# A Mamba layer and a mixture of experts on eight cores: router by quarters, three more expert units beside the scans, and the first half's sums ahead of the second half's experts

## Chip, cores and metric

One Trainium2 chip, eight NeuronCores, one sequence of 2048 tokens on each; the cores exchange nothing. The metric is the device time of the slowest core in microseconds.

## The reference

For each sequence (2048 tokens, width D = 1024):

```python
x = x + layernorm(mamba(layernorm(x)))
x = x + layernorm(moe(layernorm(x)))
# mamba: in-projection to 2 x 2048 channels, causal conv of 4 taps, silu;
#   h[t] = exp(dt[t]*A) * h[t-1] + dt[t]*x[t]*B[t]     (2048 channels x 16 states)
#   y[t] = sum over states of h[t]*C[t] + D*x[t];  y *= silu(z);  out-projection to 1024
# moe: logits = x @ router_W + router_b (15 experts); p = softmax(logits)
#   cw = p at its 3 largest entries, 0 elsewhere
#   out = relu(x @ sW1 + sb1) @ sW2 + sb2
#       + sum_e cw[:, e] * (relu(x @ eW1[e] + eb1[e]) @ eW2[e] + eb2[e])
```

## The kernel before

**Scans.** The sequence is worked in four quarters of 512 tokens, the 2048 channels in 16 groups of 128, the 16 states in fours: 64 steps a quarter, 256 in all (`LAST`). In a step ACT computes four exponentials (`dtexp`), DVE a product (`dbx`), one scan over four states (`scans`) and the product with C (`outer`), and PE adds the four states into one bank (`ysum`). Two buffers each are turned by `step % 2`. After every fourth step DVE closes a channel group (`yfin`).

**Order of the work.** All other work is placed by hand: `make_plan` puts tasks at steps, separately for each engine, and every engine runs its list strictly in order. Semaphores only make an engine wait. In a step ACT does `dtexp` first, PE `ysum` of the step before, DVE its small tasks and then the scan. In a quarter q stand the out-projection of quarter q-1 (`op`), its norms (`norm2`, `x2`, `norm3`), its transposes (`x3T`) and router logits, and the in-projections of the next quarter.

**Expert work.** A unit (`Unit`) is 256 rows through one expert's two matrices. The shared expert (number 15) has four units per half of the sequence; a routed expert (0 to 14) has one per half, of up to 256 gathered rows. A unit has eight large pieces, four `w1` (16 matmuls) and four `w2` (8 matmuls), and a routed one also two transposes of its gathered rows (`mT`). `make_units` deals the pieces to steps: `each(start, n)` gives n pieces a step before step 256 and one a step behind. Weights (four pieces of 1 MB) lie in one of four rooms (`buf`): 0 is `wa`, beside the scans the only one; 1 to 3 (`bcrep`, `xr`/`wr`, `zr`/`abv`) come free when the scans are over. A room's next weights are loaded when its last unit has used them, before step 256 on POOL's queue (L903), behind it on SP's (L706). POOL also gathers a unit's rows (`gather`, L875) and stores its output rows to `scr_y` (`store_y`, L910; L915 for shared units). ACT evicts `w2` into `ysc` (`ev_w2`, L1352), which waits until the store of the unit before has landed.

Experts 0 and 1 stand in the third quarter, 2 to 11 in the last, 12, 13 and 14 behind the scans with the last two shared units; then come the fifteen of the second half.

**Router.** It works per half of the sequence, 8 blocks of 128 tokens: `r_max` and `r_top` on DVE (L1003 to L1028: softmax, three largest, masks), `r_exp` on ACT, `rank` on PE (place of each token in its expert's list), `r_slot` on DVE (L1036 to L1050), and `scatter` on POOL (L885: 24 indirect DMAs that write token, weight and target to a slot table; L888 reads the table back into `sinfo`). In `r_top` each `max` and `max_index` waits for the one before it (`chain`).

**Sums.** `comb(h, b)` adds for a block of 128 tokens its three routed rows and the shared row (`cg`, 1 MB from `scr_y`) on PE (L1632), DVE and ACT make the norm (`st4`, `norm4`), and `fin` (L996) adds it to x2 (`xc`, 0.5 MB), which SP stores. The eight of the first half stand every three steps beside the first two experts of the second half, in two rooms and one pair of banks; those of the second half stand at the end, with three pairs of banks.

Of the kernel before, what the change touches and what calls it, by code (L numbers as in the profile page):

```python
# [15 lines left out]
D = 1024  # L16
# [10 lines left out]
HB = 8  # L27
# [38 lines left out]
def make_units():  # L66
# [80 lines left out]
def comb_steps():  # L147
    out = {}
    for b in range(8):
        out[(0, b)] = UNITS[E0].at[("w1", 0)] + 3 * b  # L150
        out[(1, b)] = END1 + 5 + b
    return out


def make_plan():
# [23 lines left out]
    for q in range(NQ + 1):  # L179
# [14 lines left out]
        if q == NQ:  # L194
            for tb in range(4):
# [13 lines left out]
            for tb in range(4):  # L209
                p.put(p.act, o + 5 + 2 * tb if tb < 2 else f + tb - 3, "norm3", q - 1, tb)  # L210
# [26 lines left out]
        if q in (2, 4):  # L237
            h = q // 2 - 1
            a = UNITS[shared(2 * q - 2)].at[("w1", 3)] + (5 if q == 2 else 6)
            b, c, d = (a + 3, a + 5, a + 6) if q == 2 else (a + 6, a + 8, a + 9)  # L240
            p.put(p.dve, a, "r_max", h)
            p.put(p.act, a + 1, "r_exp", h)
            p.put(p.dve, a + 2, "r_top", h)
            p.put(p.pe, b, "rank", h)
            p.put(p.act, b + 1, "ev_rank", h)
            for h_ in range(2 * h):
                p.put(p.pe, b, "cwT", h_)
                p.put(p.act, b + 1, "ev_cwT", h_)
            p.put(p.dve, c, "r_slot", h)
            p.put(p.pool, d, "scatter", h)  # L250
# [76 lines left out]
def build_program():  # L327
# [38 lines left out]
    with st:  # L366
# [167 lines left out]

        def usl(q, tb):
# [58 lines left out]
        LAST_F = max(n for task, n in od.f.items())  # L594


        def sp_prog(sy):
# [87 lines left out]
            def load_e(i, m, piece):  # L685
# [11 lines left out]
                else:  # L697
                    sy.wait_ge(p_y, LAST)
                    sy.wait_ge(p_f, od.f[("op", NQ - 1, 1, 3)] + 1)
                    if x.buf == 3 and m == 1:  # L700
# [30 lines left out]
            def load_cg(h, b):  # L731

                if h == 0:
                    if b < 2:
                        sy.wait_ge(p_y, LAST)
                    else:
                        sy.wait_ge(p_cb, b - 1)
# [122 lines left out]
        def pool_prog(g):  # L860
# [18 lines left out]
            def scatter(h):  # L879
                if h == 0:  # L880
                    g.wait_ge(d_zi, 32)
                g.wait_ge(v_slot, h + 1)
                for b in range(HB):
# [3 lines left out]
                g.wait_ge(d_sc, 24 * 16 * (h + 1))  # L887
                g.dma_start(sinfo[:, h], scr_si[h][0:NRT * 128, :].rearrange("(t p) c -> p t c", p=128)).then_inc(d_si, 16)  # L888
                g.wait_ge(d_si, 16 * (h + 1))
# [60 lines left out]
        def dve_prog(v):  # L950
# [48 lines left out]
            def r_max(h):  # L999
                v.wait_ge(a_tev, od.t[("logit", 2 * h + 1, 3)] + 1)  # L1000
                if h >= 1:
                    v.wait_ge(d_cw, 16 * h)
# [934 lines left out]
```

## Time and profile before

| | |
|---|---|
| median of 3 runs (lowest, highest) | 2727.54 us (2721.61, 2768.41) |
| profiled execution, time | 2716.03 us |
| its span, slowest core (cores 2698.0 to 2714.3) | 2714.3 us |
| busy: PE, DVE, ACT, POOL | 58%, 70%, 58%, 12% of the span |
| mean granted TensorE clock | 0.796 of full speed |
| HBM read and written | 202 GB/s over the span |

Busy shares are means over stages with different limits. Times within the trace count from the start of the span. A wait is put down to the semaphore that came last.

### The profile page before, as it was taken

The page shows a single profiled execution, that of the slowest core. Times are in us where ns is not written, and L with a number is a line of the kernel's source. Part 1 is how long each engine was busy: PE and PEld are TensorE (multiplying, and loading weights), DVE is VectorE, ACT ScalarE, POOL GpSimd, SP SyncE. Part 2 cuts the span into 40 slices and gives each one's busy share as a digit, 9 for nine tenths or more (in the row PEclk, how much of TensorE's full clock was granted, in tenths as well). Part 3 has the DMA queues.
Part 4 walks back from the last instruction along what each step waited for, and adds up shares of the span by engine and source line. Part 5 has one row for each costly group of instructions (what it writes and reads, how often), then busy time and mean ns, then how long its engine had stood idle before and what let it go on. Part 6 is the DMA issues. An engine that isn't in the chain of part 4 may idle for free.

```text
span 2714.3 us, 29033 instructions; the slowest of 8 cores (2698.0 to 2714.3 us)
## 1 busy us (share of the span) xinstructions
PE 1569.8 (58%) x7628; PEld 766.2 (28%) x7736; DVE 1909.0 (70%) x1490; ACT 1585.5 (58%) x2921; POOL 320.7 (12%) x290
## 2 busy tenths in 40 slices
PE   2625344543465545445645565556777777569995
PEld 1202111111132211112321232224444445326662
DVE  1197999997567999985789999979999941020003
ACT  4545666553468766546776676587777644234443
POOL 0000000000000000000007201001333203212220
PEclk9857577766787877767777788878998889689998
DMA  8399575777553443582211323242555487589975
GB/s 172 88 171 151 79 110 90 102 116 165 144 149 82 102 112 89 114 187 94 71 50 29 113 90 114 72 133 88 186 186 200 165 282 208 176 291 301 307 254 200
DMA packets 83695, 396.10 MB, mean 146 GB/s; under 512 B 21420, under 2 KB 30252, under 8 KB 55240
## 3 DMA queue, kind: packets, MB, share of 16 engines
q0 software_dynamic: 24544, 171.11, 30.0%
q1 hardware_dynamic: 58984, 223.05, 25.8%
q8 instruction: 70, 1.15, 0.2%
q14 instruction: 97, 0.79, 0.1%
HBM read 424.62 MB, written 123.64 MB: 202 GB/s over the span
## 4 chain that ended last, share of the span: by engine, by line
issue 35%; PE 22%; DMA 17%; DVE 15%; ACT 9%; POOL 1%; DVEq 1%; ACTq 0%; SPq 0%; POOLq 0%
PE ps_y L1564 6%; DVE abv L1100 6%; DVE hv L1089 4%; PE ps_c L1608 4%; PE ps_f L1479 4%; DMA xt<-x 3%; PE ps_a L1591 3%; DMA scr_y<-ysc,sinfo 3%; DMA bcrep<-scr_bc 3%; ACT abv L1374 2%; DMA wr<-scr_out 2%; DMA scr_x<-xt 2%; PE ps_f L1516 2%; DMA abv<-scr_y 1%; PE ps_f L1493 1%
## 5 line engine op out<-in xcount | busy, mean ns | idle before, releaser
L1089 DVE TENSOR_TENSOR_SCAN hv<-abv 128x2056 f16<-128x2056 f16 x256 | 1136.6, 4440 | 89.6 <-ACT abv L1374 71.4
L1374 ACT ACTIVATE abv<-ds,kc 128x512 f16<-128x512 f16 x1024 | 654.4, 710 | 72.8 <-DVE hv L1089 54.7
L1564 PE MATMUL ps_y<-abv,km 128*128 128x512 f16 x1024 | 356.1, 483 | 501.7 <-DVE abv L1100 500.1
L1079 DVE TENSOR_TENSOR abv<-ds,bcrep 128x2048 f16<-128x2048 f16 x256 | 309.2, 1208 | 51.6 <-PE ps_y L1564 27.3
L1100 DVE TENSOR_TENSOR abv<-hv,bcrep 128x2048 f16<-128x2048 f16 x256 | 312.1, 1219 | 6.4 <-DMA bcrep<-scr_bc 6.4
L1479 PE MATMUL ps_f<-xlnT,wr 128*128 128x512 bf16 x857 | 252.0, 448 | 80.2 <-ACT zr L1261 58.0
L1564 PEld LDWEIGHTS ps_y<-abv,km 128*128 128x128 f16 x1024 | 103.2, 111 | 684.4 <-issue 639.9
L986 DVE BATCH_NORM_STATS2 bst<-ps_f 128x6 f32<-128x512 f32 x11 | 7.7, 698 | 351.8 <-PE ps_f L1633 351.8
L1608 PE MATMUL ps_c<-wa,hT 128*128 128x512 bf16 x709 | 192.2, 424 | 45.8 <-ACT ysc L1352 25.4
L1340 ACT ACTIVATE hT<-ps_a,b 128x256 bf16<-128x256 f32 x304 | 126.2, 469 | 134.0 <-PE ps_a L1591 129.6
L1561 PE MATMUL ps_y<-xr,dd 128*128 128x512 f16 x64 | 32.7, 510 | 253.8 <-DVE zr L1107 253.8
L1479 PEld LDWEIGHTS ps_f<-xlnT,wr 128*128 128x128 bf16 x896 | 101.7, 115 | 234.1 <-issue 171.1
L1352 ACT ACTIVATE ysc<-ps_c,sinfo 128x512 bf16<-128x512 f32 x120 | 82.2, 686 | 146.0 <-PE ps_c L1608 92.1
L875 POOL DMA_INDIRECT xgu<-scr_x,sinfo x60 | 84.1, 1401 | 511.7 <-PE ps_t L1571 279.8
L1591 PE MATMUL ps_a<-xgu,wa 128*128 128x256 bf16 x1088 | 135.2, 285 | 2.7 <-ACT xgu L1331 1.5
L1516 PE MATMUL ps_f<-wr,zr 128*128 128x512 bf16 x435 | 112.8, 414 | 35.3 <-DMA wr<-scr_out 33.3
L1248 ACT ACTIVATE xr<-ps_f,kc 128x512 f16<-128x512 f32 x64 | 43.9, 686 | 141.5 <-PE ps_f L1493 141.5
L910 POOL DMA_INDIRECT scr_y<-ysc,sinfo x60 | 91.5, 1525 | 241.0 <-ACT ysc L1352 230.9
L937 POOL DMA_DIRECT2D scr_e<-e_w x30 | 15.1, 502 | 887.4 <-DVE abv L1100 887.4
L1591 PEld LDWEIGHTS ps_a<-xgu,wa 128*128 128x128 bf16 x1088 | 111.2, 102 | 30.1 <-issue 6.7
L1608 PEld LDWEIGHTS ps_c<-wa,hT 128*128 128x128 bf16 x736 | 77.5, 108 | 144.5 <-issue 81.2
L1074 DVE TENSOR_TENSOR ds<-ds,xr 128x512 f16<-128x512 f16 x64 | 25.9, 404 | 95.8 <-ACT ds L1366 95.8
(199 smaller groups left out, 2030.3 us busy)
## 6 DMA issues: line engine op xcount, KB each, us to landing
scr_e<-e_w POOLq DMA_DIRECT2D x30, 2048.0 KB, 19.9
wa<-scr_e POOLq DMA_DIRECT2D x56, 1024.0 KB, 6.4
wr<-scr_in SPq DMA_DIRECT2D x24, 1024.0 KB, 8.2
bcrep<-scr_e SPq DMA_DIRECT2D x24, 1024.0 KB
wa<-scr_e SPq DMA_DIRECT2D x20, 1024.0 KB
xt<-x SPq DMA_DIRECT2D x32, 512.0 KB, 5.7
bcrep<-scr_bc SPq DMA_DIRECT2D x32, 512.0 KB, 12.0
wr<-scr_out SPq DMA_DIRECT2D x14, 1024.0 KB, 7.8
```

The costliest lines, as they stand in the source:

```text
L875: g.indirect_dma_start(xg(a), None, scr_x3[x.half], bass.IndirectOffsetOnAxis(sinfo[:, x.half, 2 * x.expert + a, 0:1], 0)).then_inc(d_xg[a ...
L910: g.indirect_dma_start(scr_y[x.half], bass.IndirectOffsetOnAxis(sinfo[:, x.half, 2 * x.expert + rw, 2:3], 0), ysc[:, rw, :], None, bounds_ ...
L1079: v.tensor_mul(bv[:, step % 2, :, 2:T + 2], wdt[:, s_ % 2, :].unsqueeze(1).broadcast_to((128, 4, T)), brep[:, 4 * j:4 * j + 4, :]).then_in ...
L1089: v.tensor_tensor_scan(hv[:].rearrange("p n t -> p (n t)"), av[:, step % 2].rearrange("p n t -> p (n t)"), bv[:, step % 2].rearrange("p n ...
L1100: v.tensor_mul(bv[:, step % 2, :, 2:T + 2], hv[:, :, 2:T + 2], crep[:, 4 * j:4 * j + 4, :]).then_inc(v_hc, 1)
L1340: inst = s.activation(hT[:, hb, :], AB[c % 2][:, (hb % 2) * 256:(hb % 2 + 1) * 256], ACT.Relu, bias=b1[:, UNITS[i].expert, hb:hb + 1])
L1374: inst = s.activation(av[:, step % 2, n, 2:T + 2], dtv[:, s_ % 2, :], ACT.Exp, scale=k_a[:, g, 4 * j + n:4 * j + n + 1])
L1479: inst = t.matmul(ps[:], w[:, m, k, :], xlnT[:, k, :], start=(k == 0), stop=(k == 7))
L1516: inst = t.matmul(ps[:], zr[:, xs(q, g), tb * 128:(tb + 1) * 128], w[g // 8][:, g % 8, :], start=(g == 0), stop=(g == NG - 1))
L1564: inst = t.matmul(YB[:], k_eyh, bv[:, step % 2, n, 2:T + 2], start=False, stop=(j == 3 and n == 3))
L1591: inst = t.matmul(AB[c % 2][:, (hb % 2) * 256:(hb % 2 + 1) * 256], w[:, k, (hb % 4) * 128:(hb % 4 + 1) * 128], rows[:, k, :], start=(k == ...
L1608: inst = t.matmul(CB[rw][:], hT[:, k, rw * 128:(rw + 1) * 128], w[:, k, :], start=(k == 0), stop=(k == 7))
```

## The change

- The router works per quarter (4 blocks). Its tasks stand in the quarter behind: `scatter` at steps 91, 155, 217 and 279 instead of 155 and, for the second half, behind the scans. Within `r_top` four `max` are issued together, and four `max_index`. The slot table is read back after the second quarter of each half. The scatter of a quarter has 12 indirect DMAs.
- Experts 0 to 2 of the first half stand in the third quarter, 3 to 14 from step 213 at three pieces a step (before: 2, 2, 3), all in room 0. None is left behind the scans.
- Behind the scans come the last two shared units (steps 265 to 280, room 1), then the eight sums of the first half (281 to 288), then the fifteen experts of the second half from step 289. The transposes and norms of the last 512 tokens move up to between the last out-projections, and `x3t` of the last unit gets a room in `hv`.
- The sums have four rooms for `xc` and `cg` and three pairs of banks. SP issues the first four loads at step 265, each other one four sums later, when the result of its room is stored. `w1` of the first expert of the second half waits for all eight results (`v_out`).
- SP loads the weights of the first two second-half experts at steps 268 and 269, those of room 3 all behind the last sum.

```diff
@@ make_units
-    run([(0, e, 0, 0) for e in range(2)], each(128 + 37, 1))
+    run([(0, e, 0, 0) for e in range(3)], each(128 + 37, 1, 1, 1, 1, 2))
     run([(1, 15, 0, 0)], each(192 + 13, 2))
     run([(1, 15, 1, 0)], each(192 + 17, 2))
-    s = run([(0, e, 0, 0) for e in range(2, 12)], each(192 + 21, 2, 2, 3))
-    s = run([(0, 12, 0, 1)], each(max(s, LAST + 9), 1))
-    s = run([(1, 15, 2, 2)], each(s, 1))
-    s = run([(1, 15, 3, 2), (0, 13, 0, 0), (0, 14, 0, 1)], each(s, 1))
-    run([(1, e, 0, (0, 2, 1, 3)[e % 4]) for e in range(NE)], each(s, 1))
+    s = run([(0, e, 0, 0) for e in range(3, NE)], each(192 + 21, 3))
+    s = run([(1, 15, 2, 1)], each(max(s, LAST + 9), 1))
+    s = run([(1, 15, 3, 1)], each(s, 1))
+
+    run([(1, e, 0, (0, 2, 1, 3)[e % 4]) for e in range(NE)], each(s + 8, 1))
@@ comb_steps
-        out[(0, b)] = UNITS[E0].at[("w1", 0)] + 3 * b
+        out[(0, b)] = UNITS[E0].at[("mT", 0)] - 8 + b
@@ make_plan, last quarter, and the router
+                p.put(p.act, t + 3, "norm3", q - 1, tb)
                 f = UNITS[S14].at[("w1", 0)]
-                n = (f - 3 + tb) if tb < 2 else f + 2 + tb
+                n = o + 6 + tb if tb < 2 else f - 3 + 3 * tb
...
+        if q >= 1:
+            f = UNITS[shared(2 * q - 2)]
+            a = f.at[("w1", 3)] + 5 if q < NQ else f.at[("w1", 0)] + 9
+            p.put(p.dve, a, "r_max", q - 1)
+            p.put(p.act, a + 1, "r_exp", q - 1)
+            p.put(p.dve, a + 2, "r_top", q - 1)
+            p.put(p.pe, a + 3, "rank", q - 1)
+            p.put(p.act, a + 4, "ev_rank", q - 1)
+            p.put(p.dve, a + 5, "r_slot", q - 1)
+            p.put(p.pool, a + 5 + (q < NQ), "scatter", q - 1)
@@ banks, load_xc, load_cg
-            return FB if h == 0 else (FB, CB, AB)[b % 3]
+            return (FB, CB, AB)[b % 3]
...
+                    elif b < 4:
+                        sy.wait_ge(p_y, LAST)
+                        sy.wait_ge(p_f, od.f[("op", NQ - 1, 1, 3)] + 1)
                     else:
-                        sy.wait_ge(d_xc[b - 2], 48)
+                        sy.wait_ge(d_xc[b - 4], 48)
...
-                        sy.wait_ge(p_cb, b - 1)
+                        sy.wait_ge(p_cb, b - 3)
@@ scatter
-            def scatter(h):
+            def scatter(q):
+                h, b0 = q // 2, 4 * (q % 2)
...
-                g.wait_ge(v_slot, h + 1)
-                for b in range(HB):
+                g.wait_ge(v_slot, q + 1)
+                for b in range(b0, b0 + 4):
                     for k in range(3):
                         g.indirect_dma_start(scr_si[h], bass.IndirectOffsetOnAxis(sli[:, h, k, b:b + 1], 0),
                                              info[:, k, b, :], None).then_inc(d_sc, 16)
-                g.wait_ge(d_sc, 24 * 16 * (h + 1))
...
+                if q % 2 == 1:
+                    g.wait_ge(d_sc, 24 * 16 * (h + 1))
@@ r_top
-                for b in range(HB):
-                    chain(v.max(m8[:, b, :], pr[:, b, :]))
-                    chain(v.max_index(ix[:, b, :], m8[:, b, :], pr[:, b, :]))
...
+                for b in range(b0, b0 + 4):
+                    inst = v.max(m8[:, b, :], pr[:, b, :])
+                chain(inst)
+                for b in range(b0, b0 + 4):
+                    inst = v.max_index(ix[:, b, :], m8[:, b, :], pr[:, b, :])
+                chain(inst)
@@ w1 on PE
+                if i == E0 and c == 0:
+                    t.wait_ge(v_out, 8)
@@ SP's order behind the scans
-                            at = op_end if (u.buf, m) != (3, 1) else comb_steps()[(0, 7)] + 1
+                            at = op_end if u.buf != 3 else comb_steps()[(0, 7)] + 1
+                        if i == E0:
+                            at = UNITS[S14].at[("w1", 0)] + 3
+                        elif i == E0 + 1:
+                            at = UNITS[S14].at[("w1", 0)] + 4
...
-            put_moe(s_ - 1 if h == 0 else last_z.at[("w2", 1, 1)] + 2, "xc", h, b)
-            put_moe(s_ - 1 if h == 0 else END1 + 3, "cg", h, b)
+            soon = UNITS[S14].at[("w1", 0)] if b < 4 else comb_steps()[(h, b - 4)] + 4
+            put_moe(soon if h == 0 else last_z.at[("w2", 1, 1)] + 2, "xc", h, b)
+            put_moe(soon if h == 0 else END1 + 3, "cg", h, b)
```

## Rows read from the trace of the kernel before

**Rows 1.** DVE's timeline, closing products of two scan groups (start us, us)

```profile
2020.00 0.68 DVE L1107 TENSOR_TENSOR zr<-ps_y,zr 128x512 f16<-128x512 f32 x1
...
2048.60 0.69 DVE L1107 TENSOR_TENSOR zr<-ps_y,zr 128x512 f16<-128x512 f32 x1
```

**Rows 2.** Waits of PE, 1895 to 2180 us (total us, times, longest)

```profile
PE ps_y L1564 <- DVE abv L1100: 46.4, 24, 4.3
PE ps_y L1561 <- DVE zr L1107: 18.7, 8, 4.4
```

**Rows 3.** Windows: length, busy us (instructions) by engine, TensorE clock, DMA share, GB/s

```profile
2000.00:2050.00 50.00, 39.26 (x257) 23.82 (x258) 49.00 (x33) 39.83 (x71) 16.67 (x13) 1.00 0.53 182
...
2100.00:2150.00 50.00, 36.81 (x224) 22.26 (x224) 49.24 (x32) 33.65 (x63) 9.90 (x11) 0.88 0.55 196
...
2220.00:2250.00 30.00, 22.66 (x172) 16.18 (x175) 3.37 (x8) 16.51 (x34) 1.50 (x2) 0.83 0.98 334
...
2290.00:2330.00 40.00, 12.14 (x39) 4.50 (x41) 0.00 (x0) 4.72 (x7) 20.43 (x22) 0.62 0.40 86
...
2510.00:2530.00 20.00, 17.83 (x131) 11.77 (x131) 0.00 (x0) 8.50 (x15) 3.98 (x4) 1.00 1.00 310
```

**Rows 4.** PE's timeline: first projection, and w1 and last w2 of units

```profile
2187.57 3.61 PE L1516 MATMUL ps_f<-wr,zr 128*128 128x512 bf16 x15 [1.01 <-DVE zr L1107]
...
2349.72 2.76 PE L1591 MATMUL ps_a<-xgu,wa 128*128 128x256 bf16 x16 [1.47 <-ACT xgu L1331]
...
2468.39 7.15 PE L1591 MATMUL ps_a<-xgu,zr 128*128 128x256 bf16 x64
...
2599.73 7.15 PE L1591 MATMUL ps_a<-xgu,zr 128*128 128x256 bf16 x64
...
2655.68 6.85 PE L1608 MATMUL ps_c<-bcrep,hT 128*128 128x512 bf16 x31 [1.46 <-ACT hT L1340]
```

**Rows 5.** POOL's timeline: first and last scatter (of 24) of either router, next store

```profile
1433.78 4.91 POOL L885 DMA_INDIRECT scr_si<-info,sli  x1 [12.33 <-DVE info L1044]
...
1492.04 4.04 POOL L885 DMA_INDIRECT scr_si<-info,sli  x1 [0.30 <-issue]
...
2282.65 1.01 POOL L885 DMA_INDIRECT scr_si<-info,sli  x1 [0.30 <-issue]
...
2311.82 0.96 POOL L885 DMA_INDIRECT scr_si<-info,sli  x1 [0.30 <-issue]
...
2323.32 0.59 POOL L915 DMA_DIRECT2D scr_y<-ysc  x1 [7.16 <-DMA sinfo<-scr_si]
```

**Rows 6.** Wait of the sums; w2 pieces, y sum; DMA issues (last: us to landing)

```profile
PE ps_f L1632 <- DMA abv<-scr_y: 30.5, 5, 11.2
...
1971.29 5.30 PE L1608 MATMUL ps_c<-wa,hT 128*128 128x512 bf16 x16
1977.29 1.03 PE L1564 MATMUL ps_y<-abv,km 128*128 128x512 f16 x4 [0.70 <-DVE abv L1100]
...
wa<-scr_e POOLq DMA_DIRECT2D x56, 1024.0 KB, 6.4
...
zr<-scr_x SPq DMA_DIRECT2D x4, 512.0 KB, 26.5
```

**Rows 7.** DVE's timeline: the second half's router, borders of its three parts

```profile
2266.36 0.28 DVE L1011 TENSOR_REDUCE rsum<-pr 128x8 f32<-128x120 f32 x1 [5.71 <-ACT pr L1312]
...
2267.44 0.18 DVE L1015 MAX8 m<-pr 128x8 f32<-128x15 f32 x1
...
2268.07 0.18 DVE L1015 MAX8 m<-pr 128x8 f32<-128x15 f32 x1
...
2274.84 0.28 DVE L1028 TENSOR_TENSOR pr<-sls,pr 128x120 f32<-128x120 f32 x1
2276.61 0.22 DVE L1036 TENSOR_SCALAR slm<-rkc 128x120 f32<-128x120 f32 x1 [1.48 <-ACT rkc L1318]
...
2281.20 0.14 DVE L1050 TENSOR_SCALAR some<-big 1x1 int32<-1x1 f32 x1
```

More of the change, by code:

```diff
@@ L236, in make_plan @@
             p.put(p.act, o + 62, "siluz", q + 1, 0)
[L237 to L250, printed above, removed]
+        if q >= 1:
[8 more added lines that the diff above has]
+            p.put(p.pool, a + 5 + (q < NQ), "scatter", q - 1)
+    for h in range(2):
+        n = LAST - 26 if h == 0 else UNITS[E0].at[("w2", 0, 0)]
+        p.put(p.pe, n, "cwT", h)
+        p.put(p.act, n + 1, "ev_cwT", h)
     for step, t in PIECES:
@@ L592, in e_done @@
             return (d_ep if early(i) else d_e[UNITS[i].buf])[2 * m + piece]
-        LAST_F = max(n for task, n in od.f.items())
         def sp_prog(sy):
@@ L699, in load_e @@
                     sy.wait_ge(p_f, od.f[("op", NQ - 1, 1, 3)] + 1)
-                    if x.buf == 3 and m == 1:
+                    if x.buf == 3:
                         sy.wait_ge(p_cb, 8)
@@ L997, in fin, with r_max @@
                 inst.then_inc(v_out, 1)
[L999 to L1002, printed above, removed]
[L1003 to L1017 removed]
+            def r_max(q):
+                bs = slice(4 * (q % 2), 4 * (q % 2) + 4)
+                v.wait_ge(a_tev, od.t[("logit", q, 3)] + 1)
+                if q >= 2:
+                    v.wait_ge(d_cw, 16)
+                chain(v.reduce_max(nmx[:, bs], lg[:, bs, :], AX.X, negate=True))
+                v.tensor_add(pr[:, bs, :], lg[:, bs, :], nmx[:, bs].unsqueeze(2).broadcast_to((128, 4, NE))
+                             ).then_inc(v_rmx, 1)
@@ new lines, in r_top @@
+            def r_top(q):
+                h, b0 = q // 2, 4 * (q % 2)
+                bs = slice(b0, b0 + 4)
+                v.wait_ge(a_rex, q + 1)
+                if q >= 1:
+                    v.wait_ge(p_t, od.t[("rank", q - 1)] + 1)
+                chain(v.reduce_sum(rsum[:, bs], pr[:, bs, :], AX.X))
+                chain(v.reciprocal(rsum[:, bs], rsum[:, bs]))
+                chain(v.tensor_mul(pr[:, bs, :], pr[:, bs, :], rsum[:, bs].unsqueeze(2).broadcast_to((128, 4, NE))))
+                if q >= 2:
+                    v.wait_ge(d_si, 16)
+                for b in range(b0, b0 + 4):
[4 more added lines that the diff above has]
+                chain(inst)
+                chain(v.tensor_copy(ixf[:, bs, :], ix[:, bs, 0:3]))
@@ L1023, in r_top @@
[L1023 to L1038 removed]
+                chain(v.tensor_add(sls[:, bs, :], oh[:, 0, bs, :], oh[:, 1, bs, :]))
@@ new lines, in r_top, with r_slot @@
+                chain(v.tensor_add(sls[:, bs, :], sls[:, bs, :], oh[:, 2, bs, :]))
+                v.tensor_copy(mk[:, bs, :], sls[:, bs, :]).then_inc(v_msk, 1)
+                v.memset(cwm[:, h, bs, 15:16], 1.0)
+                v.tensor_mul(cwm[:, h, bs, 0:NE], sls[:, bs, :], pr[:, bs, :]).then_inc(v_cw, 1)
+                v.wait_ge(v_cw, q + 1)
+                v.tensor_mul(pr[:, bs, :], sls[:, bs, :], pr[:, bs, :]).then_inc(v_cwf, 1)
+            def r_slot(q):
+                h, b0 = q // 2, 4 * (q % 2)
+                bs = slice(b0, b0 + 4)
+                v.wait_ge(a_tev, od.t[("rank", q)] + 1)
+                v.wait_ge(v_cw, q + 1)
+                v.wait_ge(v_cwf, q + 1)
+                rank = rkc[:, 0:128].rearrange("p (b e) -> p b e", e=16)[:, bs, 0:NE]
+                chain(v.tensor_scalar(slm[:, bs, :], rank, CAP - 0.5, 8192.0, AL.is_gt, AL.mult))
+                chain(v.tensor_add(sls[:, bs, :], rank, k_ios.unsqueeze(1).broadcast_to((128, 4, NE))))
+                chain(v.tensor_max(slm[:, bs, :], slm[:, bs, :], sls[:, bs, :]))
@@ L1584, in w1 @@
                     t.wait_ge(a_fev, od.f[("x3T", n // 2, 2 * (n % 2) + 1)] + 1)
-                rows = xgT if x.routed else x3t
+                rows = xgT if x.routed else x3r(4 * x.half + x.part)
                 if 4 * i + c >= 2:
```

142 lines of the change are left out of this document (65 added, 77 removed).

## The prediction, made before the changed kernel ran

> **What bounds the kernel now.** I read the page's 40 slices, then the windows by stage, then the timeline of each engine around the stage borders, then the waits. They show three stages.
>
> Up to about 2187 us the state scans run, and DVE sets the pace. In the last quarter four scan steps take 28.6 us, 7.15 us a step [rows 1], without a gap. PE is not full: in 285 us it waits 46.4 and 18.7 us for DVE, some 1.65 us a step [rows 2], though a window there has it busy 39.3 of 50 us [rows 3].
>
> From the first output projection (2187.57) to the first expert matmul of the second half (2349.72) are 162.1 us [rows 4]. PE does seven units of work there, but for 40 us it is busy 12 [rows 3]: POOL scatters the second half's routing between 2282.65 and 2312.8, reloads the slot table and only at 2323.3 stores the next expert output [rows 5]. ACT waits for that store before it may overwrite `ysc`, and PE waits for ACT.
>
> From 2349.72 to 2662.5 run the fifteen experts of the second half, 312.8 us. The last twelve have nothing between them: eight of them take 131.3 us (16.42 each, DMA share 1.00 and 310 GB/s), the last four 62.8 (15.7 each) [rows 3, 4]. The first three take 118.7 us, because eight sums (`comb`) of the first half stand between them, and PE waits 30.5 us for their data [rows 4, 6]. Then come 51.8 us of the second half's sums.
>
> **Part 1: routers beside the scans.** Before, one 8-block router (first half) lies beside the scans and one behind. Afterwards three 4-block ones lie beside them and one behind. An 8-block router costs DVE 0.7 us (`r_max`, two of its instructions), 8.8 (`r_top`, 2266.36 to 2275.1) and 4.7 (`r_slot`, 2276.61 to 2281.3), 14.2 together [rows 7]. In it each block's max and index take 0.63 us with their waits, 5.0 for eight. With 14 of 16 waits gone I take the bare 0.44 us (0.18 plus 0.26), 1.8 for four. The other 9.2 us are waits and tiny instructions at half the elements: between half (4.6) and unchanged (9.2); I take 7.2, near unchanged, since 0.18 us for 15 elements beside 0.28 for 120 is mostly fixed cost. So 9.0 us each (6.4 to 11.7), 27 for three, less the 14.2 removed: **+13 us** (+5 to +21) on the bound engine.
>
> **Part 2: the scatter of the third quarter on POOL's queue.** It stands at step 217, in the middle of dense units. Beside scans 24 scatters took from 1433.8 to 1496.1, 2.6 us each; behind them 24 took 30.1, 1.26 each [rows 5]. So 12 take about 31 us, started as scan 216 starts (call this 0). Behind them on POOL stand the two output stores of unit 9, the last weight piece of unit 10 and gathers and weights of unit 11. ACT's eviction of unit 10 (step 219) waits for unit 9's store to land, and stands on its engine ahead of the exponentials for scan 220, which is due at 28.6. Scatters end at 32 (quicker once DVE stalls), store issued at 34, landed about 38, eviction 0.7, exponentials 4.3: scan 220 starts at 43. **+14 us**. Unit 10's last weights, issued at 36 and landing in the usual 6.4 us [rows 6], come at the same moment. Bounds: 0 if scatters go at 1.26 us (15 us in all is covered), 25 if also the weights behind run late. The same scatter at step 91 and the shorter one at 155 have no near unit behind them: nothing.
> The Trainium skill (SBUF — State Buffer, "SBUF: two separate sides") has DVE and GpSimd share a port pair under an exclusive lock, so that GpSimd can't write descriptors while certain DVE operations run, and gives 620 ns grown to about 3100. The trace agrees in kind: scatters of 4 to 4.9 us stand among those of 0.96. By the page's figure for all twelve POOL would be blocked 41 us, and the stall some 7 us longer.
>
> **Part 3: three more units beside the scans.** One of them is in the third quarter, where PE waits more. In steps 213 to 252 there are 12 units for 10, three pieces a step. PE needs 12 x 15.7 for units, 41 for the y sums of 40 steps (1.03 each [rows 6]) and 14 for the z projections: 244 of 286 us at full clock. The 1.65 us of waiting a step shrink to about 0.6. Where z projections stand (8 steps) a step needs 7.1, all there is, but PE may lag 3.4 us before DVE feels it. I take **+4 us** (0 to +30; the upper end if every step of that stretch slips by the missing eviction latency of 0.8 us).
> Sum of the scan stage: **+31 us**, so the first output projection starts at 2218.6.
>
> **Part 4: from there to the second half's experts, 132 instead of 162 us.** Call the start 0. Eight projections of 3.5 us [rows 4] and two waits for the norms (no unit covers them now: transposes are due between them) end at 33; PE comes out of a pause, so add 3 for half clock. The two shared units, 14 us each, run to about 68 with the router between them. Its chain: last logit 51, exp 55, `r_top` to 60, rank, `r_slot` to 66, 12 scatters of 1.26 us to 81, reload (before: 11.5 us from the last scatter to the next store) to 93, gathers and transposes: 104. That alone would let the experts start at 104.
> But `w1` of the first one now also waits for all eight sums, and these wait for transfers. A sum reads 1.57 MB. SP issues four sums' loads at 28 to 34, then weights of units 23 and 24 (8.4 MB), of 25 (4.2), then four results (2.1), each of which must have landed before its room takes the next sum's 1.57 MB. With the last four sums' loads (6.3), a part of the first four's, stores and gathers some 31 MB must pass after 34. Direct loads ran at 334 GB/s [rows 3]: 93 us, so the last sum's data land at 127, plus product, statistics and result (8 us) is 135; some 3 MB may have passed before 34, hence **132**. Bounds: 104 if the sums are never late, 150 if landing round trips leave queue gaps of 3 us each. An SP transfer behind weights did land late before: 26.5 us for the 0.5 MB of `zr<-scr_x` [rows 6].
> The Trainium skill (DMA: Bandwidth & Descriptors, "Queues, rings and completion order") has the queue rows served in turn by packets and a ring's descriptors consumed in order. So small loads on POOL's queue would get past SP's weights, and the sums' loads on SP's own would not; both are as I reckon here.
> Gain: **30 us**. The old 40 us hole is gone, since no unit with a `ysc` store stands behind the scatter but unit 22's own.
>
> **Part 5: fifteen experts without sums between them.** The state at their start is that of 2468: three weight rooms full, the fourth loading. So 11 at 16.42 and 4 at 15.7: 243.4 us for 312.8, **-69 us**. Bounds: 236 (all 15.7) to 258 (17.2, where DMA at 305 GB/s carries a unit's 5.24 MB). The end, 51.8 us, is not touched.
>
> **Sum.** +31 -30 -69 = -68 us. The profiled execution has a span of 2714.3 and a time of 2716.0: 2648. The three runs' median is 11.5 us above that execution and their lowest 5.6; I add 6: **2654 us**.
>
> **Rivals.**
> A. *The sums are not late; the router's chain sets the start (104).* For: DMA share was only 0.40 in the old hole, queues can run empty. Against: 31 MB. It gives 28 us less, 2626.
> B. *Transfers and density take more*: start at 150, a unit 17.2 us or the scan stage another 15 us: 2654 + 18 + 15, about 2687. For: share 1.00 in all late windows. Against: 12 units did run at 16.2 in it.
> C. *Slower: PE becomes the bound of the last scan quarter.* One mechanism: half clock. Two w2 pieces took 5.3 us at a low clock against 3.4 [rows 6]. 244 us of work fill the 286 at a mean clock of 0.86; below that the scans wait for the y sums. All 99 us gained behind the scans, less the 27 of parts 1 and 2, are lost at 244/c = 286 + 72, c = 0.68; at 0.65 the time is about 2740. For: 0.88 in one window before [rows 3]. Against: PE kept 1.00 in the densest window, and denser work leaves fewer pauses.
> D. *The scatter does not hold up the scans*, because POOL gets its port during other DVE gaps: 14 us less, 2640; inside my range.
>
> **Chances and range.** Forecast with D 0.52, A 0.17, B 0.24, C 0.07. Range 2600 to 2710: A with some of the other lower bounds, B with the upper bound of part 3. A measurement of this kernel tells about 2% from no change; that is 2673 and 2782. The forecast falls to "within 2%" in a sixth of its cases, A never, B mostly: faster 0.63, same 0.32, slower 0.05.
>
> **What would show it.** Right: the first projection near 2219; three router groups of about 9 us on DVE beside scans; one DVE wait of 10 to 20 us for ACT's exponentials near step 220; PE idle ahead of sums 4 to 7 on DMA; first expert at 130 us behind the first projection, and waiting for a result of DVE, not for the gather; experts at a pitch of 15.7 to 16.6 us with DMA at 1.00. Wrong: many small DVE waits for PE's y sums in the last quarter (C), experts starting with their gather (A), or a pitch above 17 us (B).

## The result, and the profile after

The changed kernel took 2696.9 us (median of five runs) beside 2721.6 us for the kernel before on the same chip: ratio 0.9906, 95% interval 0.9877 to 0.9935. It is 25 us faster where 73 were forecast. That lies inside the range of 2600 to 2710, but short of the 2% that the chance of 0.63 stood on. One of the five executions of either kernel, and some of the experiments', were in a slower state, in which the cores of one die show a lower clock; the ratios, and the times of the experiments below, leave these out.

The granted clock and the span of three of the cores, after the change, first:

```profile
core 0: 2657.4 us, clock 0.795
...
core 4: 2695.1 us, clock 0.792
...
core 6: 2654.4 us, clock 0.798
```

Before, the eight spans lay between 2698.0 and 2714.3; now they lie between 2654.4 and 2695.1. The mean core gained 32.2 us (2706.2 to 2674.0), the slowest 19.2. The clock did not move (0.796 before and 0.792 after on the slowest core). Since the cores of one run already differ by up to 30 us at scan 84, where both kernels are the same, I read the stretches below as means over the eight cores. "Scans 212 to 224" is from the start of one scan to that of the other; "first sum" (its first matmul), "last sum" (start of its second product) and "first expert" (first `w1` of unit 23) count from the core's first output projection of the last quarter; "units" is from the first expert to the last `w2`.

| us, mean of 8 cores | before | after | difference |
|---|---|---|---|
| scans 84 to 96 (router of quarter 0) | 85.6 | 93.8 | +8.2 |
| scans 144 to 160 (router of quarter 1; before, of the half) | 149.8 | 144.3 | -5.5 |
| scans 212 to 224 (router and scatter of quarter 2) | 85.7 | 111.4 | +25.7 |
| scans 224 to 255 | 220.9 | 228.9 | +8.0 |
| first projection | 2182.2 | 2215.1 | +32.9 |
| from there to the last sum | 265.5 | 156.0 | |
| from there to the first expert | 164.9 | 166.2 | +1.3 |
| units | 308.1 | 241.9 | -66.2 |
| tail of PE's work | 38.1 | 37.3 | -0.8 |

So the scans lost about what was forecast (+33 for +31), the experts gained what was forecast (-66 for -69), and the stretch between them, from which 30 us were to come, gave nothing. A part of the +33 is chance: from scan 84 to scan 255 the kernel after takes 36.7 us more, but its cores reached scan 84 3.8 us earlier (843.3 for 847.1), up to where both kernels are the same.

**The scans.** POOL's timeline of core 4 at scan 216, start and length in us, operation, and in brackets the idle time before and its releaser:

```profile
1923.09 1.53 POOL L898 DMA_INDIRECT scr_si<-info,sli  x1 [0.30 <-issue]
1924.93 4.56 POOL L898 DMA_INDIRECT scr_si<-info,sli  x1 [0.30 <-issue]
...
1949.04 0.96 POOL L898 DMA_INDIRECT scr_si<-info,sli  x1 [0.31 <-issue]
1950.31 1.00 POOL L925 DMA_INDIRECT scr_y<-ysc,sinfo  x1 [0.30 <-issue]
...
1956.37 0.58 POOL L918 DMA_DIRECT2D wa<-scr_e  x1
```

ACT's timeline in the same place:

```profile
1956.62 0.69 ACT L1384 ACTIVATE ysc<-ps_c,sinfo 128x512 bf16<-128x512 f32 x1 [15.26 <-DMA scr_y<-ysc,sinfo]
```

PE's timeline, where the weights issued by POOL behind the stores are late too:

```profile
1960.49 3.57 PE L1646 MATMUL ps_c<-wa,hT 128*128 128x512 bf16 x8 [13.76 <-DMA wa<-scr_e]
```

DVE's timeline, with the product that the next scan group begins with:

```profile
1958.90 0.42 DVE L1101 TENSOR_TENSOR ds<-ds,xr 128x512 f16<-128x512 f16 x1 [15.98 <-ACT ds L1398]
```

This is Part 2 as forecast: twelve scatters take 27 us, the store of unit 9's output is issued at 1950.3, ACT's eviction waits for its landing until 1956.6, and DVE, which had no gap in [rows 1], stands 16 us for ACT. The scatters took between 0.96 and 4.56 us, as in [rows 5], and ended in a row of 0.96 once DVE stood still. What holds a long one is seen beside DVE's scan:

```profile
1931.12 4.44 DVE L1116 TENSOR_TENSOR_SCAN hv<-abv 128x2056 f16<-128x2056 f16 x1
```

```profile
1932.15 4.17 POOL L898 DMA_INDIRECT scr_si<-info,sli  x1 [0.30 <-issue]
```

Three scatters were begun while a scan ran (1924.93, 1932.15, 1939.17), and each ended 0.8 us behind the end of that scan (1928.69, 1935.56, 1942.91).

Behind scan 224 DVE stands three more times for PE, which it never did there before the change. Here it is on core 2, PE's timeline and then DVE's:

```profile
2062.32 4.42 PE L1646 MATMUL ps_c<-wa,hT 128*128 128x512 bf16 x10 [5.23 <-DMA wa<-scr_e]
```

```profile
2071.16 1.23 DVE L1106 TENSOR_TENSOR abv<-ds,bcrep 128x2048 f16<-128x2048 f16 x1 [5.76 <-PE ps_y L1600]
```

PE comes late with the y sum, because it waited for weights (`wa`) that POOL issued. This happens near steps 225, 235 and 245 on most cores; DVE's waits of this kind are 3.5 us in the mean of the cores (0.6 to 8.4; 1 us more is a wait at the same instruction on cores 4 and 7 to which the profile gives no releaser). With 2.0 us for ACT just behind step 235 on every core and about 1 us of shorter waits they make up the +8.0.

**The gap between scans and experts.** PE's timeline of core 4, from the first projection to the first expert:

```profile
2231.50 5.50 PE L1548 MATMUL ps_f<-wr,zr 128*128 128x512 bf16 x15 [1.40 <-DVE zr L1134]
...
2278.36 3.57 PE L1629 MATMUL ps_a<-x3t,bcrep 128*128 128x256 bf16 x16 [4.45 <-ACT hT L1372]
...
2361.61 1.87 PE L1665 MATMUL ps_c<-abv,km 128*128 128x512 bf16 x4 [27.97 <-DMA abv<-scr_y]
...
2385.26 1.25 PE L1665 MATMUL ps_c<-zr,km 128*128 128x512 bf16 x4 [2.49 <-DMA zr<-scr_y]
...
2397.27 9.93 PE L1629 MATMUL ps_a<-xgu,wa 128*128 128x256 bf16 x64 [1.46 <-ACT xgu L1363]
```

SP's DMA queue in the same time (weights, first results, and the loads that stand behind them):

```profile
2283.80 2.70 SPq L713 DMA_DIRECT2D wa<-scr_e  x4
2286.70 5.36 SPq L713 DMA_DIRECT2D xr<-scr_e  x2
...
2307.16 11.58 SPq L713 DMA_DIRECT2D bcrep<-scr_e  x2
2328.61 3.47 SPq L761 DMA_DIRECT2D out<-ds  x2
2352.99 0.33 SPq L739 DMA_DIRECT2D ds<-scr_x  x1
...
2369.43 0.34 SPq L761 DMA_DIRECT2D out<-xr  x1
2369.96 0.32 SPq L739 DMA_DIRECT2D zr<-scr_x  x1
...
2375.83 0.34 SPq L761 DMA_DIRECT2D out<-ds  x1
2376.36 0.32 SPq L739 DMA_DIRECT2D xr<-scr_x  x1
```

and the windows (length, busy us and instructions of PE, its weight loads, DVE, ACT and POOL, TensorE clock, DMA share, GB/s):

```profile
2300.00:2320.00 20.00, 17.36 (x107) 8.04 (x108) 6.41 (x35) 4.94 (x13) 9.21 (x10) 0.91 0.98 224
2320.00:2340.00 20.00, 6.74 (x18) 1.55 (x16) 8.96 (x18) 6.64 (x13) 4.07 (x4) 0.61 1.01 320
2340.00:2360.00 20.00, 0.00 (x0) 0.00 (x0) 0.00 (x0) 0.00 (x0) 3.12 (x4) 0.50 0.93 258
2360.00:2380.00 20.00, 10.45 (x25) 2.50 (x25) 6.04 (x12) 3.70 (x8) 0.00 (x0) 0.59 0.76 253
2380.00:2400.00 20.00, 11.26 (x46) 4.96 (x47) 7.44 (x14) 5.61 (x10) 1.89 (x2) 0.59 0.71 216
2400.00:2500.00 100.00, 93.12 (x693) 64.57 (x698) 0.00 (x0) 48.98 (x87) 23.87 (x24) 0.99 0.99 314
```

Result 0 is issued at 2328.61, behind 12.6 MB of weights (units 23, 24 and 25) on the same queue. Until it has landed its room may not take sum 4's input, and that load is next in SP's order: it goes out at 2352.99, 24.4 us later. PE, DVE and ACT do nothing at all between 2340 and 2360. What follows is a chain of round trips, not a stream: 8.6 us until sum 4 can start (2361.61), then result 3, which `fin` writes on DVE behind the statistics of sum 4. DVE's timeline:

```profile
2366.13 0.70 DVE L1001 BATCH_NORM_STATS2 bst<-ps_c 128x6 f32<-128x512 f32 x1 [28.80 <-PE ps_c L1666]
...
2367.95 1.41 DVE L1011 SCALAR_TENSOR_TENSOR xr<-ps_f,mv,xr 128x512 f32<-128x512 f32 x2
```

so it is issued at 2369.43, with sum 6's load behind it. Sum 7's load needs result 3's room, but that had landed at 2372.44; what it waits for is its turn on SP behind result 4, which DVE finished only at 2375.75, behind the statistics of sum 5. It goes out at 2376.36 and takes 8.9 us (2385.26). The DMA share falls to 0.76 and 0.71: here the queues wait, the bytes don't.

The router's chain was slower too. POOL's timeline behind the scans, to set beside the last lines of [rows 5]:

```profile
2333.34 1.68 POOL L902 DMA_DIRECT2D sinfo<-scr_si  x1 [10.34 <-issue]
...
2347.92 1.12 POOL L930 DMA_DIRECT2D scr_y<-ysc  x2 [12.90 <-DMA sinfo<-scr_si]
```

POOL waits 10.3 us between the last scatter and the reload, which may not start before the scatters have landed, and 12.9 for the table; before, the table took 7.16 [rows 5].

### The profile page after: what moved, and what is told of

It is laid out like the page before. It is cut to its first block, busy times and chain, and to the rows that moved or that the text cites. A ratio compares the mean times of both kernels' runs of the same rounds, so it can differ in the third digit from the quotient of the medians.

```text
span 2695.1 us, 29141 instructions; the slowest of 8 cores (2654.4 to 2695.1 us)
## 1 busy us (share of the span) xinstructions
PE 1561.3 (58%) x7632; PEld 762.5 (28%) x7736; DVE 1914.5 (71%) x1546; ACT 1585.9 (59%) x2925; POOL 369.7 (14%) x302
## 4 chain that ended last, share of the span: by engine, by line
issue 32%; PE 23%; DMA 17%; DVE 14%; ACT 10%; POOL 1%; DVEq 1%; ACTq 0%; SPq 0%; another core or an unknown queue 0%; POOLq 0%
PE ps_y L1600 6%; DVE abv L1127 5%; PE ps_a L1629 5%; DVE hv L1116 4%; PE ps_f L1511 4%; DMA scr_y<-ysc,sinfo 4%; DMA xt<-x 4%; PE ps_c L1646 3%; ACT abv L1406 2%; PE ps_f L1548 2%; DMA wr<-scr_out 2%; DMA bcrep<-scr_bc 2%; DMA scr_x<-xt 1%; DMA wa<-scr_e 1%; DVE h_last L1125 1%
## 5 line engine op out<-in xcount | busy, mean ns | idle before, releaser
L1646 PE MATMUL ps_c<-wa,hT 128*128 128x512 bf16 x773 | 200.3, 411 | 47.4 <-DMA wa<-scr_e 25.2
L887 POOL DMA_INDIRECT xgu<-scr_x,sinfo x60 | 99.3, 1656 | 473.9 <-PE ps_t L1607 319.4
L1629 PE MATMUL ps_a<-xgu,wa 128*128 128x256 bf16 x1216 | 145.1, 279 | 5.9 <-ACT xgu L1363 2.9
L1548 PE MATMUL ps_f<-wr,zr 128*128 128x512 bf16 x435 | 117.7, 429 | 36.7 <-DMA wr<-scr_out 33.8
L1629 PEld LDWEIGHTS ps_a<-xgu,wa 128*128 128x128 bf16 x1216 | 120.8, 100 | 32.2 <-issue 9.3
L925 POOL DMA_INDIRECT scr_y<-ysc,sinfo x60 | 101.9, 1699 | 160.6 <-ACT ysc L1384 148.4
## 6 DMA issues: line engine op xcount, KB each, us to landing
bcrep<-scr_bc SPq DMA_DIRECT2D x32, 512.0 KB, 12.5
```

The source lines that it names most:

```text
L887: g.indirect_dma_start(xg(a), None, scr_x3[x.half], bass.IndirectOffsetOnAxis(sinfo[:, x.half, 2 * x.expert + a, 0:1], 0)).then_inc(d_xg[a ...
L925: g.indirect_dma_start(scr_y[x.half], bass.IndirectOffsetOnAxis(sinfo[:, x.half, 2 * x.expert + rw, 2:3], 0), ysc[:, rw, :], None, bounds_ ...
L1548: inst = t.matmul(ps[:], zr[:, xs(q, g), tb * 128:(tb + 1) * 128], w[g // 8][:, g % 8, :], start=(g == 0), stop=(g == NG - 1))
L1629: inst = t.matmul(AB[c % 2][:, (hb % 2) * 256:(hb % 2 + 1) * 256], w[:, k, (hb % 4) * 128:(hb % 4 + 1) * 128], rows[:, k, :], start=(k == ...
L1646: inst = t.matmul(CB[rw][:], hT[:, k, rw * 128:(rw + 1) * 128], w[:, k, :], start=(k == 0), stop=(k == 7))
```

## The experiments

Theory A: the sums' loads are held in SP's order, behind result 0 and result 3. Theory B: transfers as such (bytes) set the end, wherever they stand. For the scans: the scatter on POOL's queue (12 to 16 us) against denser units.

**e1: the third quarter's scatter behind the scans** (it loses no order that a reader of it needs; the table of the half is read only there).

```
-p.put(p.pool, a + 5 + (q < NQ), "scatter", q - 1)
+p.put(p.pool, LAST - 2 if q == 3 else a + 5 + (q < NQ), "scatter", q - 1)
```

> The changed kernel with one edit: the 12 scatters of the third quarter stand at step 254 instead of 217, behind the last unit's output stores. Theory (POOL's queue holds up the scans): the 16.6 us that steps 216 to 220 lost against the kernel before shrink to under 3 us, scan 255 starts 14 to 18 us earlier (near 2206 instead of 2222), all behind it moves up unchanged, time 14 to 18 us shorter, about 2680. Rival (the loss at these steps comes from the denser units, and the scatter only stands beside it): scan 255 moves by less than 5 us, time unchanged.

Measured: scans 212 to 224 take 98.9 us for 111.4, the first projection is at 2202.1 for 2215.1, everything behind it nearly as in after (first expert 168.1 for 166.2). Two executions took 2682.1 and 2699.2 us, without an interval, so the stretches carry the reading: the scatter cost 12.5 us, a little less than the 14 to 18 expected. DVE's wait of 16 us fell, in the timeline of e1's slowest core, to

```profile
1940.05 0.42 DVE L1101 TENSOR_TENSOR ds<-ds,xr 128x512 f16<-128x512 f16 x1 [1.43 <-ACT ds L1398]
```

Scans 224 to 255 stayed at 230.0: their 8 us are no echo of the scatter.

**e2: sums 4 to 7 four steps later**, so that result 3 is written before sum 4's statistics stand on DVE.

```
-run([(1, e, 0, ...) for e in range(NE)], each(s + 8, 1))
+run([(1, e, 0, ...) for e in range(NE)], each(s + 12, 1))
-out[(0, b)] = UNITS[E0].at[("mT", 0)] - 8 + b
+out[(0, b)] = UNITS[E0].at[("mT", 0)] - 12 + b + 4 * (b >= 4)
```

> The changed kernel with sums 4 to 7 and all behind them four steps later in the written order (no work added), so that on DVE the results of sums 0 to 3 no longer stand behind the statistics of sum 4, and SP can store them. Theory A (SP's queue order alone: the first result lands 24 us late behind expert weights): the hole ahead of sum 4 stays near 28 us, and the first expert starts at most 5 us earlier than 165.8 us behind the first projection. Theory B (the circle result 3 - statistics of sum 4 - loads of sum 6 on SP adds to it): the hole ahead of sum 4 stays, but sum 7 comes 12 to 16 us earlier and the first expert starts near 152 us.

Measured: one run, 2687.0 us; first expert 161.1 for 166.2. The order on DVE costs 5 us, no more. (Kernels that are the same in this stretch agreed within 2 us: 166.2 in after and 168.1 in e1, 138.9 in both e5 and e6.)

**e3: weights of units 24 and 25 issued behind the last sum's loads.** The same bytes, in another order on SP's queue.

```
 elif i == E0 + 1:
-    at = UNITS[S14].at[("w1", 0)] + 4
+    at = comb_steps()[(0, 7)]
+elif i == E0 + 2:
+    at = comb_steps()[(0, 7)]
```

> The changed kernel with SP's loads of the weights of units 24 and 25 (8.4 MB) moved behind the loads of the last sum; order of the sums as in the changed kernel. Theory A (results of the sums land late behind 8.4 MB of weights on the same queue): result 0 lands within 8 us instead of 24, the hole ahead of sum 4 falls from 28 to under 10 us, the first expert starts at 135 to 145 us behind the first projection instead of 165.8, then set by the router's chain or the circle on DVE. Rival C (the router's chain sets the start, with the gathers issued at 118 us): no earlier than 160. Rival D (DMA volume sets it): weights only move behind, the first two experts then wait for their weights by what was gained, and the end stays within 8 us.

Measured: one run, 2678.8 us; last sum at 139.3 for 156.0, first expert 149.5 for 166.2, units 244.4 for 241.9. PE's wait for sum 4 fell from 27.97 us, in PE's timeline of e3, to

```profile
2342.85 1.86 PE L1665 MATMUL ps_c<-abv,km 128*128 128x512 bf16 x4 [11.45 <-DMA abv<-scr_y]
```

On that core sum 4's load went out 3.7 us behind the issue of result 0, where it took 24.4 before. Just short of what was expected (135 to 145), with the same bytes in another order: theory A for 17 us, and B is out. No run put the weights on another queue, so whether result 0 landed late by its place in SP's queue or because all queues were full stays open; e3 shows that issuing 8.4 MB later mends it.

**e4: e2 and e3 together.**

> Both edits of the two kernels above. If they are independent links of one chain of transfers: first expert at 120 to 132 us behind the first projection, set by the router's chain (slot table, gather, transposes), and the time 30 to 40 us shorter than the changed kernel's. If volume is the bound: the expert starts earlier but waits for weights, time at most 15 us shorter.

Measured: 2678.3 us, ratio 0.981 (0.972 to 0.990); first expert 144.2, the sum of both gains (22.0 for 5.1 + 16.7), not the 120 to 132 that was expected. The time is 19 us under after's, where 30 to 40 were expected. Units 246.9: 5 us are given back, since three rooms of weights are no longer full at their start; on the slowest core PE waits 8.3 us there for weights, in after not at all.

**e5: eight rooms for eight sums.** Sums 4 to 7 get memory that is idle by then (`xlnT`, `xt`, `xr`, `wr`), so that no load waits for a result; weights of units 24 and 26 wait for the sums.

```
+if b >= 6:
+    return xt[:, b - 6, :]
+if b >= 4:
+    return xlnT[:, 4 * b - 16:4 * b - 12, :]...
...
-    sy.wait_ge(d_xc[b - 4], 48)
+    sy.wait_ge(v_x2, 16)
```

> The changed kernel with eight rooms instead of four for the first half's sums (xc 4 to 7 in xlnT and xt, cg 4 to 7 in xr and wr), all loads issued by step 268, so that no load waits for a result to land; in exchange the weights of unit 24 (room 2) load behind the sums, as those of unit 26 do. Theory (the start of the second half's experts was set by round trips of room reuse on SP's queue): PE never waits ahead of sums 4 to 7 for data, the last sum starts at 105 to 115 us behind the first projection instead of 156, and the first expert at 120 to 130 us instead of 166.2, now set by the router's chain (gathers issued near 115). Units take 3 to 8 us more (245 to 250 us), time 30 to 38 us under the changed kernel's. Rival (volume of transfers): the sums' data still come late, first expert not before 145 us, time at most 20 us shorter.

Measured: 2676.3 us, ratio 0.9834 (0.9809 to 0.9859). The last sum is at 109.0, as expected, and none waits for data any more. But the first expert is at 138.9 where 120 to 130 was expected: behind the sums stands now what the sums had hidden. So the time is 21 us under after's, not the 30 to 38 expected.

**e6: e5 and e1 together.**

> Eight rooms for the sums, and the 12 scatters of the third quarter at step 254 instead of 217. Both causes removed, they lie in different stages: the gains add, 13 us in the scans (mean of the cores, as measured with the scatter alone) and 30 to 38 behind them: 43 to 50 us under the changed kernel, about 2650, ratio to the kernel before near 0.973. If they share a cause, the sum is less than 35.

Measured: 2663.7 us, ratio 0.9785 (0.976 to 0.981), less than expected but faster than both kernels: scans 212 to 224 99.5, first expert 138.9. The total, 33 us under after, is below the 35 that I had named as the sign of a common cause, but by stretches both gains are there in full (12 us in the scans as in e1, 27 to the first expert as in e5); it was e5's own gain that I had put too high. What holds the first expert is seen in PE's timeline of its slowest core, whose sums ended near 2342:

```profile
2357.20 1.01 PE L1615 MATMUL ps_t<-km,xgu 128*128 128x128 bf16 x8 [14.84 <-DMA xgu<-scr_x,sinfo]
```

and in POOL's:

```profile
2304.73 1.00 POOL L906 DMA_INDIRECT scr_si<-info,sli  x1 [11.05 <-DVE info L1077]
...
2318.31 0.96 POOL L906 DMA_INDIRECT scr_si<-info,sli  x1 [0.27 <-issue]
2328.65 1.68 POOL L910 DMA_DIRECT2D sinfo<-scr_si  x1 [9.38 <-DMA scr_si<-info,sli]
2343.16 1.12 POOL L938 DMA_DIRECT2D scr_y<-ysc  x2 [12.83 <-DMA sinfo<-scr_si]
2344.56 1.00 POOL L895 DMA_INDIRECT xgu<-scr_x,sinfo  x1 [0.29 <-issue]
```

This is rival A's chain (scatter, table, gather), at 139 us and not at 104.

**e7: unit 14 left behind the scans**, in after otherwise; what one unit beside the scans costs there, and saves.

```
-run([(0, e, 0, 0) for e in range(3, NE)], each(192 + 21, 3))
+run([(0, e, 0, 0) for e in range(3, NE - 1)], each(192 + 21, 3))
+run([(0, NE - 1, 0, 0)], each(max(s, LAST + 9), 1))
```

> The changed kernel with expert 14 of the first half taken from beside the scans and put behind them, ahead of the two shared units; 11 instead of 12 units at three pieces a step. If the denser units themselves cost the scans the 8 us of steps 224 to 255 evenly, these steps take 226 to 228 us instead of 228.9 (220.9 before). If the loss comes from single late stores and weights in POOL's queue, it stays at 228 to 230. In either case the first sum comes 12 to 17 us later behind the first projection, since the unit needs 15.7 us there, and the time is 10 to 15 us longer than the changed kernel's: the price of one unit left behind.

Measured: one run, 2737.4 us, 40 more than after where 10 to 15 were expected. Scans 224 to 255 take 230.3, not less: the 8 us there are not an even price of density. The first sum comes 22.4 us later (104.2; 12 to 17 were expected) and the first expert 36.9 (203.1). On the slowest core sum 4's load goes out 34.5 us behind the issue of result 0 (2358.45 to 2392.90), 10 us more than in after. PE's timeline of e7, at sum 4:

```profile
2400.20 1.86 PE L1666 MATMUL ps_c<-abv,km 128*128 128x512 bf16 x4 [43.13 <-DMA abv<-scr_y]
```

Taking one unit away from beside the scans gave them nothing back, and behind them it cost, as this kernel is ordered, more than twice its own 16 us.

**e8, e9, e10: is the router's chain slow because the queues are full?** Theory S: yes; rival F: an indirect write and a table of small rows take that long by themselves. e8 is e6 with unit 25's weights issued behind the last sum; e9 moves unit 23's as well (8.4 MB out of the chain's way); e10 is e8 again, for its time.

```
 e8:  +elif i == E0 + 2:
      +    at = comb_steps()[(0, 7)] + 1
 e9:  -if i == E0:
      -    at = UNITS[S14].at[("w1", 0)] + 3
      -elif i == E0 + 2:
      +if i in (E0, E0 + 2):
```

> Kernel: e6 with one thing moved: the 4.2 MB of weights of unit 25 (the third expert of the second half) are issued behind the last sum, after those of unit 24, and no longer while the router's chain runs. What sets the first expert at 139 us behind the first projection in e6 is POOL's chain: last scatter issued, 9.4 us until it has landed, 12.8 us for the table, then some 12 us to the gathered rows. Before the change, in a window where the DMA engines were busy 0.40, the same two waits took 1.7 and 7.2 us. Theory S: the saturated queues (share 0.96 to 1.00) lengthen them, so with 4.2 MB less in the way (13 us at 320 GB/s) the share falls below 0.9 for some 10 us, the two waits fall by 5 to 10 us together and the first expert starts at 127 to 134 (mean of the cores). Rival F: the landings' length has nothing to do with SP's weights (a fixed latency of an indirect write and of small rows): waits stay at 9 and 13 us, first expert at 137 to 140. Either way the units may take 1 to 4 us more (246 to 250), since a room is filled later, so the total moves by less than 0.3%: ratio 0.975 to 0.979.

> Kernel: e8, and the 4.2 MB of unit 23 (the first expert of the second half) issued behind the last sums as well, so that 8.4 MB less than in e6 run beside the router's chain. It is made to see POOL's two waits, mean of the eight cores: behind the last scatter (3.4 us before the change, 10.6 in e6, 9.7 in e8) and for the table (7.4, 13.8, 11.0). Theory S (saturated queues lengthen them): e8 left the DMA share near 1.00 in most cores, so it shortened them little; with 25 MB of transfers between 35 and 115 us cut to 17 MB (0.65 of what 320 GB/s carry) the waits fall to at most 7 and 9, gathers are issued at 105 to 112 instead of 117 to 121. Rival F (a fixed latency): 9 to 11 and 11 to 14, gathers as in e8. The first expert itself then waits for unit 23's weights, which are issued at about 105 and need 13 us and more: it starts at 125 to 138 by S, 130 to 145 by F, and unit 24's weights come later, so the units may take 2 to 6 us more. Ratio 0.972 to 0.981.

> Kernel: e8 unchanged, for its time, since its first three rounds gave no interval. By the stretches of its trace (first projection at 2203.9, first expert 133.6 behind it, units 243.7, mean of the cores) it should be 7 to 8 us under e6 and 0.3% under it: ratio 0.973 to 0.978, about 2650 us. If the 5 us that the first expert gained are only noise between runs, the ratio is 0.978 and more.

| us, mean of 8 cores | before | after | e6 | e8 | e9 |
|---|---|---|---|---|---|
| POOL's wait behind the last scatter | 3.4 | 11.0 | 10.6 | 9.7 | 3.5 |
| its wait for the table | 7.4 | 12.3 | 13.8 | 11.0 | 6.9 |
| first gather | | 119.4 | 121.1 | 117.1 | 106.8 |
| first expert | 164.9 | 166.2 | 138.9 | 133.6 | 125.3 |
| units | 308.1 | 241.9 | 246.1 | 243.7 | 254.8 |

POOL's timeline of e9's slowest core:

```profile
2306.89 0.96 POOL L906 DMA_INDIRECT scr_si<-info,sli  x1 [0.27 <-issue]
2311.12 1.68 POOL L910 DMA_DIRECT2D sinfo<-scr_si  x1 [3.27 <-DMA scr_si<-info,sli]
2319.83 1.12 POOL L938 DMA_DIRECT2D scr_y<-ysc  x2 [7.03 <-DMA sinfo<-scr_si]
```

and the windows of that core at the same time:

```profile
2290.00:2310.00 20.00, 18.21 (x76) 6.37 (x74) 11.62 (x35) 8.09 (x17) 11.57 (x12) 1.00 0.61 223
2310.00:2330.00 20.00, 8.44 (x33) 2.52 (x31) 14.37 (x28) 9.08 (x20) 4.78 (x5) 0.80 0.82 192
```

With DMA shares of 0.61 and 0.82 both waits are back where they were before the change, where the share was 0.40 [rows 3]. Theory S holds, and F is out: the two waits are 24.4 us in e6 and 10.4 in e9. e8 alone would not have told it: it left the share near 1.00, and the waits fell by 3.7 us where S wanted 5 to 10, though the first expert came at 133.6, within S's 127 to 134. e9 itself gives 8.7 of its 13.6 us back, for the units start with empty rooms and take 254.8; two executions took 2645.5 and 2646.5 us, without an interval. e8 starts the first expert later and keeps its units short: as e10 it took 2647.7 us, ratio 0.9741 (0.9716 to 0.9766), with the first expert at 134.0 again. e9 and e10 can't be told apart (2631.1 and 2631.4 us in the mean of their cores); both are under e6 (2639.7).

## Why the prediction was wrong

- **Part 1 (routers, +13).** Right. `r_max`, `r_top` and `r_slot` of four blocks took 0.5, 4.4 and 3.8 us, 8.8 for 9.0. By stretches +8.2 and -5.5, and some 8 of the +25.7, 11 in all.
- **Part 2 (scatter, +14).** Right in size and by its own steps; e1 took 12.5 us away. Rival D is out: POOL did not find its gaps. The Trainium skill's page "SBUF — State Buffer", section "SBUF: two separate sides", has its lock between DVE and GpSimd; the trace agrees in kind, with scatters of 4.17 to 4.56 us that end 0.8 us behind a scan, and of 0.96 as soon as DVE stood. The 7 us more that its figure would have made were not there: the stall was 16 on the slowest core.
- **Part 3 (density, +4).** Low: about 13 (8.0 behind scan 224, and 5 of the 25.7, which is the difference to parts 1 and 2), inside its bounds. (Its 0.6 us of waiting left a step is 42 us over 40 steps, so 1.05; the sum doesn't use it.) e1 and e7 show that it is neither the scatter's echo nor even. From 1895 to 2200 PE waits 25.2 us for weights in POOL's queue, where it waited for none before:

```profile
PE ps_c L1646 <- DMA wa<-scr_e: 25.2, 4, 13.8
```

  13.8 of them belong to the scatter. The others are the waits near steps 225, 235 and 245, behind each of which DVE stands for the late y sum. That they go away with earlier weights wasn't tried.
- **The stage as a whole.** Parts of 13, 14 and 4 were forecast, and some 11, 12.5 and 13 came: 36.7 us for 31. That the first projection stood at +33 is due to the cores' 3.8 us at scan 84, by luck.
- **Rival C.** Out as it was meant: the clock from scan 213 to 255 was 0.90 to 0.93 on the eight cores, before 0.89 to 0.92. But its sign, DVE waiting for y sums, did appear, for 3.5 us in the mean behind scan 224, and came from late weights.
- **Part 4 (132 instead of 162).** This is the step that failed: 166. It priced the sums' data as a volume, 31 MB at 334 GB/s, in which each transfer moves up when its turn comes. SP's queue was not a volume but an order with holds in it. (1) Sum 4's load stood behind the landing of result 0, and that behind 12.6 MB of weights issued shortly before; moving 8.4 of them gave 17 us back in e3. (2) Results 3 and 4, with loads behind them on SP, stood behind the statistics of sums 4 and 5 on DVE: 5 us by e2, which takes only result 3 out of this. I had even written that each result "must have landed before its room takes the next sum's 1.57 MB", and had put queue gaps of 3 us each into the upper bound. The one hold behind result 0 was 24.4 us, and loads then took 8.6 and 8.9 us until their sum could start, one behind the other. The upper bound of 150 was too low for that. Of the 34 us that were missed, 27 are the sums' (e5 has the first expert at 138.9) and 7 the router's chain. The sum itself had a slip too: 3 MB at 334 GB/s are 9 us, so its own terms give 126 and not 132, further off.
- **Part 4, the router's chain (104).** Wrong as well, and hidden by the sums. e9, with everything else out of its way, starts the first expert at 125. On e9's slowest core its steps read: last projection done at 39 (36 in my chain), last logit at 64 (51), first scatter at 79 (66), last one begun at 92 (80), table there at 105 (93), first `w1` at 124 (104). So the router began 13 us late: 3 us were lost in the projections, and about 10 in the first shared unit, in which the last two transposes stand and PE waits 4.5 us for `hT` (the first product's output, which ACT writes); and gathers, transposes and evictions took 19 us and not 11. With full queues the two landings add 14 us more (24.4 in e6 for 10.4 in e9): 139, as in e5 and e6. I had reckoned that POOL's small transfers get past SP's weights; they took more than twice as long beside them. So even with sums that are never late the forecast of 132 was out of reach for the kernel as it was written, and rival A's 28 us were worth nothing.
- **Part 5 (units, -69).** Right: -66.2, at 16.1 us a unit with the DMA share at 0.99 in 2400 to 2500.
- **The mark of the first expert.** I had it waiting for a result of DVE. On PE it waits for ACT's copy of the transposed rows; these transposes stand behind the last sum in PE's order. The last sum set the time all the same.
- **The core.** All terms were reckoned on the core that ended last. By the mean of the cores the result is -32.2 us, which is the sum of the table (+32.9 +1.3 -66.2 -0.8 = -32.8); the measure takes the slowest, and the spread went from 16 to 41 us. Why it grew isn't settled.

## What to carry to other kernels

When a queue works in order and one of its transfers waits for a room, reckon the time to that point from the landing of what frees the room, with all bytes issued ahead of it, and only then add bytes: 8.4 MB of weights that nobody needed yet, issued 42 to 10 us before a 0.5 MB result, cost 17 us here, and e3 had them back by order alone. A small, serial chain of DMAs (scatter, table, gather) pays for full queues with its latency at each link, so bulk loads that can wait go behind it, but no more of them than the next stage can do without: e9 started its first expert 8.3 us before e8 and took 11.1 us more for the units. And when one thing is late, work out what would be next without it before counting the gain; here it was 139 us behind 166, where I had believed 104.

## What was not expected of the hardware

- POOL's two waits, for twelve indirect writes to land and for the table of small rows, were 10.4 us together at DMA shares of 0.6 to 0.8 (e9), and 23 to 24 us at 0.9 and more (after, e6).
- Twelve scatters beside scans cost DVE more than the router of the same quarter does (8.8 us): 16 us on the slowest core, 12.5 in the mean. One that was begun beside a scan took 4.2 to 4.6 us and ended 0.8 us behind the scan's end; most others took 0.96.
- The first projection behind the scans took 5.50 us for 15 matmuls, one some 30 us later 3.61 for 16: part of it ran at the lower of the clock's two levels. The granted clock was 0.61 of full speed from 2231 to 2237 and 1.00 from 2237 to 2245; in the 26 us ahead PE had been busy 11.6 us, with waits of some 4 us for DVE. I had put 3 us in for that; the projections ended another 3 us later.
- The cores drifted apart by up to 30 us in the first 850 us of one execution, though they all do the same work.
